# A selective scan on one NeuronCore: sums of y placed by a table, ScalarE's rows of B's diagonals in other steps, one GpSimd build a triple earlier

## The chip, the cores and the metric

The kernel runs on one core of one Trainium2 chip. The metric is the device time of one execution in microseconds (us). The kernel before took 1583.36 us, the median of three runs (1574.06 to 1601.38). The profiled execution, from which all rows below come, took 1595.89 us.

## The reference, cut to what matters

The model is one vision-Mamba block and one mixture-of-experts block on an input of 4 x 32 x 32 x 384. The change touches only the selective scan of the first block. With 192 channels, 16 states, 1024 positions and 4 directions, the reference computes for each image and direction

```python
def step(h, inp):
    u_t, d_t, B_t, C_t = inp
    dA = jnp.exp(d_t[..., None] * As)
    h = h * dA + (d_t * u_t)[..., None] * B_t[:, :, None, :]
    y = jnp.einsum('bkcn,bkn->bkc', h, C_t)
    return (h, y)
```

where d is softplus of a projection of the input (dt), u the convolved input, and B and C projections of it. Directions 2 and 3 run backwards, directions 1 and 3 over the transposed image. The outputs of the four directions are added into one y per image; then come a layer norm, a gate, a projection and the experts.

## The kernel before, in words

**Three stages.** A head (normalisation, projection, convolution; up to about 188 us of the span), the scan (`scan`, about 188 to 1315 us), and a tail (projection and experts). Only the scan is touched.

**Units and steps.** The scan works through 16 units, one for each image (4), orientation (2) and direction of flow (2); `unit_of` gives the three. A unit has 24 steps: 8 pairs of states, called triples here because each takes three steps (`CG = 3`), one for each group of 64 channels by 2 states by 1024 positions. So step i of a unit belongs to triple i // 3, part i % 3. "Step 3" in this text is step 3 of a unit, "unit 6" is the seventh. In one step:

- TensorE's `spread_b` (matmuls of line 1018) writes the term dt * u * B of the step into one of two PSUM buffers `s_pb`: 32 matmuls, 64 instructions, of the stationary dt * u with a diagonal matrix that holds B. It waits until the scan two steps back has ended (`h_ready`).
- ScalarE's `decay` (line 1109) writes exp(dt * A) into one of four buffers `s_a`, two steps ahead.
- VectorE's `step_h` (line 1183) does the scan itself, h = a * h + b along 1024 positions, into a ring of four triples of `s_h`.
- GpSimd's `times_c` (line 1219) multiplies h by C's row, two parts of a triple in one instruction and the third in another, in place.
- TensorE's `add_y` (line 1058) adds the products into y in PSUM (`s_py`, `s_py2`): the "sum" of the step. It waits for GpSimd (`hc_ready`) and for the sum before it. A slot of the ring is free for the scan when its sums are done (`y_added`).

**Order on each engine.** Each engine runs its instructions in program order, so the loops in the blocks of `scan` are the schedule: what waits holds all that stands behind it on the same engine. On TensorE, step i is: spread of step i, then the sums due by the function `summed`, then a carry if one is due, then the chunk of the next unit if one is due.

**Sums.** `summed(u, i)` says how many sums are done after step i of unit u: all up to seven steps back (`LAG = 7`). In even units after the first, `BEHIND` holds one or two more back in steps 7 to 12. This makes one sum a step, none in steps 7 and 8 of an even unit, two in steps 10 and 13 there.

**Carries.** At the middle of an image (after its first two units, one orientation), VectorE's `take_y` copies y out with the skip term (lines 1174 and 1175, after the scan of step 6), and TensorE adds it back transposed in six pieces, `carry` (lines 1028 and 1035), at the places of `CARRIES`: pairs of unit % 4 and step. At the end of an image ScalarE's `take_y` (line 1114 and the one after it, in step 6 of the next image's first unit) copies y out and SyncE's `store_y` stores it, in its queue behind the load of C's row for triple 3 and ahead of that for triple 4.

**Chunks.** During a unit, the inputs of the next are made: TensorE writes a chunk into the one bank `m_pm`, ScalarE takes it. Z chunks (dt before softplus, line 224) in steps 0 to 3, BT (line 228) in step 4, UT (u transposed, lines 237 and 239; only for even next units, so during odd ones) in steps 5, 7, 10 and 13, DUP (dt per channel group, line 245) in steps 16 to 19. The dt chunk of the prediction is the Z chunk. Softplus is done in three rounds from steps 7, 10 and 13 (`ROUND_AT`): ScalarE's logarithm (line 1095) into `m_pm`, then VectorE's two operations after the scan of the step (lines 1157 and 1160) and two after the next (1163 and 1166). After the scan of step 15 VectorE multiplies dt by u (`times_u`, line 308).

**Diagonals of B.** The 16 diagonal matrices of a unit stand in `k_area` in four quarters ("pieces"), which spreads read in steps 0 to 5, 6 to 11, 12 to 17 and 18 to 23. ScalarE builds pieces 0 and 2 a row at a time (`build_rows`, line 298; 32 rows of a piece): piece 0 of the next unit in steps 6 to 17, the first half of its piece 2 in steps 18 to 23, the second half in steps 0 to 5 of the unit itself, two or three rows a step. GpSimd builds pieces 1 and 3 in one instruction each (`build_d`, line 204): piece 3 of the unit behind triple 1, piece 1 of the next unit behind triple 4.

Of the kernel before, what the change touches and what calls it, by code (L numbers as in the profile page):

```python
# [40 lines left out]
BLK = 8  # L41
# [1 line left out]
CROWS = 3  # L43
TRIPLES = 4
LAG = 7
BEHIND = {LAG: 1, LAG + 1: 2, LAG + 2: 2, LAG + 3: 1, LAG + 4: 1, LAG + 5: 1}
CARRIES = {(2, 11): 0, (2, 12): 1, (2, 14): 2, (2, 15): 3, (3, 8): 4, (3, 11): 5}
ROUND_AT = (7, 10, 13)
ROUNDS = 3
AHEAD = 2  # L50
LN2 = 0.693147
LOG_MAX = 80.0
Y_STORED = 16 * 3
# [851 lines left out]
def scan(nc, d, keep, ys, m, norm, shared):  # L905

    with ExitStack() as ctx:
# [94 lines left out]
        @block.tensor  # L1002
        def _(pe):
            def spread_b(u, i):

                n, g = i // CG, i % CG
                step = u * STEPS + i
                if i == 0:
                    pe.wait_ge(dtu_ready, u + 1)
                if i % 6 == 0:  # L1010
                    piece = i // 6
                    pe.wait_ge(d_odd if piece % 2 else d_even, 2 * u + piece // 2 + 1)
                need(pe, h_ready, step - 1)
                for blk in range(BLK):
                    for r in range(2):
                        here = slice(r * HALF, (r + 1) * HALF)
                        for par in range(2):
                            mm = pe.matmul(pb[par * HALF:(par + 1) * HALF, step % 2, r * BANK + blk:(r + 1) * BANK:BLK],  # L1018
                                           dtut[here, u % 2, blk, g * HALF:(g + 1) * HALF], dd[here, 2 * n + par, blk],
                                           start=True, stop=True)  # L1020
                mm.then_inc(b_row, 1)

            def carry(b, piece, made):

                pe.wait_ge(y_added, made)
                if piece < 4:
                    q, w = halves()[piece // 2], piece % 2
                    mm = pe.matmul(py[:, q].rearrange("p (w h) -> p w h", h=HW)[:, w * HW // 4:(w + 1) * HW // 4], eye[:],
                                   y01[:].rearrange("p (h w) -> p w h", w=HW)[:, piece * HW // 4:(piece + 1) * HW // 4],
                                   start=False, stop=False)  # L1030
                else:
                    for x in range(2):
                        lh = x ^ (piece - 4)
                        here, cols = slice(lh * HALF, (lh + 1) * HALF), slice(x * HW // 2, (x + 1) * HW // 2)
                        mm = pe.matmul(py2[x * HALF:(x + 1) * HALF].rearrange("p (w h) -> p w h", h=HW)[:, :, lh * HW // 2:(lh + 1) * HW // 2],
                                       eye[here, here], y2[here].rearrange("p (h w) -> p w h", w=HW)[:, cols], start=False, stop=False)
                mm.then_inc(y_carried, 1)
                pe.wait_ge(y_carried, len(CARRIES) * b + piece + 1)

            def add_y(n, part):  # L1040

                b, o, s = unit_of(n // NP)
                first, last = n % (2 * NP) == 0, n % (2 * NP) == 2 * NP - 1
                if first and part == 0:
                    need(pe, y_taken, 2 * taken(b, o))
                at = n % TRIPLES * CG
                pe.wait_ge(hc_ready, 2 * n + (1 if part == 0 else 2))
                need(pe, y_added, CG * n + part)
                for r in range(2):
                    here = slice(r * HALF, (r + 1) * HALF)  # L1050
                    into = (part + r) % CG
                    opens, closes = first and part == (0, 0, 1)[into], last and part == (2, 1, 2)[into]
                    for x in range(2):
                        if into < 2:
                            dst, src = py[x * HALF:(x + 1) * HALF, halves()[into]], h[here, at + x, halves()[into]]
                        else:
                            dst, src = py2[x * HALF:(x + 1) * HALF], h[here, at + 2, halves()[x]]
                        mm = pe.matmul(dst, eye[here, here], src, start=opens, stop=closes)  # L1058
                mm.then_inc(y_added, 1)

            def summed(u, i):

                held = u > 0 and u % 2 == 0
                return max(0, u * STEPS + i + 1 - LAG - (BEHIND.get(i, 0) if held else 0))

            for u in range(UNITS):
                for i in range(STEPS):
                    step = u * STEPS + i
                    spread_b(u, i)
                    made = summed(u, i)  # L1070
                    for at in range(summed(u, i - 1), made):
                        add_y(at // CG, at % CG)
                    if (u % 4, i) in CARRIES:
                        carry(u // 4, CARRIES[u % 4, i], made)
                    if u + 1 < UNITS:
                        for what in chunks_of(u + 1):
                            if chunk_slot(*what) == i:
                                m.chunk(pe, u + 1, *what)
                    elif 6 <= i < 6 + TT:
                        t = i - 6  # L1080
                        if t == 0:
                            pe.wait_ge(norm.y_in, 16)
                            pe.wait_ge(chunk_taken, len(CHUNK))
                        need(pe, norm.yt_taken, t)
                        norm.turn(pe, pm, t)
            for step in range(LAST - LAG, LAST):
                add_y(step // CG, step % CG)

        @block.scalar
        def _(act):  # L1090
            def logarithm(u, r):
# [1 line left out]
                act.wait_ge(chunk_taken, CHUNK[u, "BT", 0] + 1 + (r + 2 if u % 2 == 0 else 0))  # L1093
                need(act, dt_ready, ROUNDS * u + r)
                nc.scalar.activation(pm[:], ez[:, round_cols(r)], ACT.Ln, bias=1.0).then_inc(ln_ready, 1)

            def share(k):

                return 4 * BLK * k // 12

            def decay(step):
                u, i = step // STEPS, step % STEPS
# [17 lines left out]
            for u in range(UNITS):  # L1120
                b, o, s = unit_of(u)
                for i in range(STEPS):
                    step = u * STEPS + i
                    if step + AHEAD < LAST:
                        decay(step + AHEAD)
                    if i == 6 and s == 0 and o == 0 and u:
                        take_y(b - 1)
                    if u + 1 < UNITS:
                        for what in chunks_of(u + 1):
                            if chunk_slot(*what) == i:  # L1130
                                m.take_chunk(act, u + 1, *what)
                        if 4 <= i < 6:
                            m.exponent(act, u + 1, i - 3)
                        if i in ROUND_AT:
                            logarithm(u + 1, ROUND_AT.index(i))
                        if 6 <= i < 18:
                            m.build_rows(act, u + 1, 0, share(i - 6), share(i - 5))
                        if i >= 18:
                            m.build_rows(act, u + 1, 2, share(i - 18), share(i - 17))
                    if i < 6:  # L1140
                        m.build_rows(act, u, 2, share(i + 6), share(i + 7))
                    if u == LAST_U and 6 <= i < 6 + TT:
                        norm.take(act, pm, 0, i - 6).then_inc(norm.yt_taken, 1)
            norm.root(act, 0)
# [4 lines left out]
        def _(dve):  # L1149
# [36 lines left out]
            for u in range(UNITS):  # L1186
                b, o, s = unit_of(u)
                for i in range(STEPS):
                    step_h(u * STEPS + i)
                    if i == 6 and s == 0 and o == 1:  # L1190
                        take_y(b)
                    if u + 1 < UNITS:
                        for r, at in enumerate(ROUND_AT):
                            if at <= i < at + 2:
                                softplus(u + 1, r, 2 * (i - at))
                                softplus(u + 1, r, 2 * (i - at) + 1)
                        if i == 15:
                            m.times_u(dve, u + 1)
                    if u == LAST_U and i == 0:
                        nc.vector.memset(norm.eps[:], 1e-5).then_inc(norm.eps_ready, 1)  # L1200
                    if u == LAST_U and 8 <= i < 8 + TT:
# [11 lines left out]
        def _(pool):  # L1213
# [8 lines left out]
            for u in range(UNITS):  # L1222
                for n in range(NP):
                    times_c(u * NP + n, range(0, 2))
                    times_c(u * NP + n, range(2, CG))
                    if n == 1:
                        m.build_d(pool, nc.gpsimd.tensor_tensor, u, 3)
                    if n == 4 and u + 1 < UNITS:
                        m.build_d(pool, nc.gpsimd.tensor_tensor, u + 1, 1)


# [661 lines left out]
```

## Time and profile before

| | busy us | share of the span |
|---|---|---|
| span of the profiled execution | 1594.1 | (execution: 1595.89) |
| PE, TensorE matmul | 1351.7 | 85% |
| DVE, VectorE | 1229.5 | 77% |
| POOL, GpSimd | 1025.6 | 64% |
| ACT, ScalarE | 1018.5 | 64% |
| line 1183, the 384 scans | 862.4 | 2275 ns each |
| line 1219, the products with C | 880.1 | 3468 ns each |
| line 1018, spreads | 479.2 | 226 ns a matmul instruction |
| line 1058, sums | 431.7 | 614 ns a matmul instruction |

How to read it: shares are over the whole span, of which the scan is some 1120 us. A busy time of matmuls that follow each other without a gap overlaps, because each instruction's time holds its fill and drain; for TensorE the distance from one start to the next says more than the durations. The rows of a timeline merge equal instructions that follow each other; the brackets tell how long the engine was idle before them and which engine's work ended that; "issue" stands where no releaser is seen. The granted clock of TensorE is given as a share: 1.00 is 2.4 GHz, 0.50 is 1.2 GHz. Units 1 to 14 are the stretch from 263.61 to 1244.45 us.

### The profile page before, as it was taken

The numbers are of one execution on the slowest core, as the hardware profiler recorded it, in microseconds if no ns is written. First come the engines' busy times: TensorE is split into PE (matmuls) and PEld (weight loads), VectorE is DVE, ScalarE is ACT, GpSimd is POOL, SyncE is SP. The second block draws the span as 40 slices with busy tenths as digits, with TensorE's granted clock in tenths as the row PEclk, the third lists the DMA queues.
The fourth block names the chain that finished last, engine by engine and source line by source line (L and its number), as shares of the span: only waits on it lengthen the run. The fifth ranks groups of instructions, "written<-read, shape, count | busy, mean of one in ns | idle before, by whom it ended". The sixth has DMA issues, their size and how long they took to land. (4 is left out here: it accounts for less than half of the span.)

```text
span 1594.1 us, 66411 instructions
## 1 busy us (share of the span) xinstructions
PE 1351.7 (85%) x30388; PEld 830.5 (52%) x30388; DVE 1229.5 (77%) x1029; ACT 1018.5 (64%) x1957; POOL 1025.6 (64%) x294
## 2 busy tenths in 40 slices
PE   6997688888987888998788899878889886969998
PEld 5734455554554555555555555545555543535554
DVE  4876198989899898989989997997989884644220
ACT  3448677777778778787877877776787551311222
POOL 0002089989899998999899998988899980000000
PEclk8998879999999999999999999998999997789999
DMA  9243524233333423333342332334243326100111
GB/s 324 97 156 145 170 56 112 76 93 82 81 87 89 109 79 93 79 90 81 89 113 78 91 99 70 85 85 109 66 101 80 97 82 221 67 0 35 40 40 45
DMA packets 73479, 151.13 MB, mean 95 GB/s; under 512 B 33238, under 2 KB 41942, under 8 KB 72816
## 3 DMA queue, kind: packets, MB, share of 16 engines
q1 hardware_dynamic: 73200, 146.88, 32.1%
q8 instruction: 240, 3.93, 1.1%
q14 instruction: 39, 0.32, 0.1%
HBM read 101.76 MB, written 32.51 MB: 84 GB/s over the span
## 5 line engine op out<-in xcount | busy, mean ns | idle before, releaser
L1219 POOL TENSOR_TENSOR s_h<-s_h,s_crow 128x2048 f32<-128x2048 f32 (+1 forms) x256 | 880.1, 3468 | 159.3 <-DVE s_h L1183 159.3
L1183 DVE TENSOR_TENSOR_SCAN s_h<-s_a,s_pb 128x1024 f32<-128x1024 f32 x384 | 862.4, 2275 | 131.7 <-PE s_pb L1018 96.3
L1018 PE MATMUL s_pb<-k_area,m_dtut 64*64 64x64 f32 x24576 | 479.2, 226 | 149.6 <-DVE s_h L1183 98.7
L1018 PEld LDWEIGHTS s_pb<-k_area,m_dtut 64*64 64x64 f32 x24576 | 435.4, 139 | 325.1 <-DVE s_h L1183 161.9
L1058 PE MATMUL s_py<-s_h,k_eye 64*64 64x512 f32 x3072 | 431.7, 614 | 14.6 <-issue 8.3
L298 ACT ACTIVATE k_area<-k_mask,m_bt 128x64 f32<-128x64 f32 x992 | 273.3, 337 | 0.0
L1109 ACT ACTIVATE s_a<-y_y,m_aneg 128x1024 f32<-128x1024 f32 x192 | 219.0, 1142 | 54.1 <-DVE s_h L1183 53.9
L1109 ACT ACTIVATE s_a<-m_dup,m_aneg 128x1024 f32<-128x1024 f32 x192 | 219.3, 1143 | 32.5 <-DVE s_h L1183 32.5
L204 POOL TENSOR_TENSOR k_area<-m_bt,k_mask 128x2048 f32<-128x2048 f32 x33 | 145.0, 4396 | 128.9 <-ACT m_bt L273 128.9
L1058 PEld LDWEIGHTS s_py<-s_h,k_eye 64*64 64x64 f32 x3072 | 93.2, 138 | 41.4 <-issue 35.6
L270 ACT COPY y_y<-m_pm 128x384 f32<-128x384 f32 x60 | 28.8, 479 | 79.0 <-PE m_pm L224 79.0
L224 PEld LDWEIGHTS m_pm<-k_wdt,k_rows 25*128 25x128 f32 x256 | 43.2, 199 | 59.7 <-issue 59.3
L224 PE MATMUL m_pm<-k_wdt,k_rows 25*128 25x192 f32 x256 | 63.7, 372 | 7.2 <-DMA k_rows<-scratch_xd 7.2
L1504 PE MATMUL t_small<-t_w,k_area 128*128 128x384 f32 x192 | 69.1, 497 | 0.0
L1478 PE MATMUL t_big<-t_xn,t_w 128*128 128x512 f32 x144 | 68.2, 625 | 0.0
L1568 ACT COPY t_out<-t_small 128x384 f32<-128x384 f32 x32 | 15.3, 479 | 82.4 <-PE t_small L1507 82.4
L819 DVE SCALAR_TENSOR_TENSOR h_acc<-h_xpad,h_conv_p,h_acc 128x1024 f32<-128x1024 f32 x48 | 61.7, 1285 | 1.6
L245 PEld LDWEIGHTS m_pm<-k_eye,y_y 64*64 64x64 f32 (+1 forms) x512 | 33.5, 123 | 52.7 <-issue 47.2
L1692 DVE TENSOR_TENSOR k_area<-k_area,t_big 128x1024 f32<-128x1024 f32 x12 | 14.3, 1220 | 47.9 <-PE t_big L1492 47.7
L1504 PEld LDWEIGHTS t_small<-t_w,k_area 128*128 128x128 f32 x192 | 36.5, 194 | 18.2 <-issue 1.2
L245 PE MATMUL m_pm<-k_eye,y_y 64*64 64x64 f32 (+1 forms) x512 | 43.0, 224 | 2.9 <-ACT y_y L273 2.7
L1478 PEld LDWEIGHTS t_big<-t_xn,t_w 128*128 128x128 f32 x144 | 27.8, 200 | 32.4 <-issue 31.9
(190 smaller groups left out, 1234.3 us busy)
## 6 DMA issues: line engine op xcount, KB each, us to landing
s_crow<-scratch_xd SPq DMA_DIRECT2D x256, 256.0 KB, 4.1
k_area<-in_x_dram SPq DMA_DIRECT2D x4, 1536.0 KB, 7.9
scratch_xt<-y_y SPq DMA_DIRECT2D x4, 1536.0 KB, 8.6
y_y<-y_y SPq DMA_DIRECT2D x24, 256.0 KB, 4.3
m_dup<-m_dup SPq DMA_DIRECT2D x24, 256.0 KB, 4.2
out_dram<-t_out SPq DMA_DIRECT2D x32, 192.0 KB, 1.9
k_area<-scratch_xt SPq DMA_DIRECT2D x3, 1536.0 KB, 6.8
scratch_xd<-h_dbl SPq DMA_DIRECT2D x8, 512.0 KB, 2.6
```

What stands on the lines that cost most here:

```text
L204: tt(self.dd[:, rows_n].rearrange("p n k j -> p (n k) j"), self.bt[:, u % 2, rows_n].rearrange("p n k -> p (n k)").unsqueeze(2).broadcast_ ...
L224: mm = pe.matmul(pm[:, x * DI:(x + 1) * DI], tokens(rows[0:R + 1], 2 * i + x), self.keep["wdt"][:, o + 2 * s], start=True, stop=True)
L245: mm = pe.transpose(pm[0:chans.stop - chans.start, blk::BLK], self.dt_of[here, blk, chans], eye[here, here])
L298: row = self.nc.scalar.activation(self.dd[:, n, blk], self.keep["mask"][:], ACT.Identity, scale=self.bt[:, u % 2, n, blk:blk + 1])
L819: eng.scalar_tensor_tensor(out, view, w, out, ALU.mult, ALU.add).then_inc(convolved[kind], 1)
L1018: mm = pe.matmul(pb[par * HALF:(par + 1) * HALF, step % 2, r * BANK + blk:(r + 1) * BANK:BLK], dtut[here, u % 2, blk, g * HALF:(g + 1) * H ...
L1058: mm = pe.matmul(dst, eye[here, here], src, start=opens, stop=closes)
L1109: nc.scalar.activation(a[:, step % RING], dup[u % 2][:, g], ACT.Exp, scale=aneg[:, col:col + 1]).then_inc(a_ready, 1)
L1183: nc.vector.tensor_tensor_scan(h[:, step % (TRIPLES * CG), f], a[:, step % RING, f], pb[:, step % 2, f], 0.0, ALU.mult, ALU.add).then_inc( ...
L1219: nc.gpsimd.tensor_tensor(here, here, c.unsqueeze(1).broadcast_to([P, groups.stop - groups.start, L]), ALU.mult).then_inc(hc_ready, 1)
L1478: mm = pe.matmul(big_of("F1", b, j)[:, q], w1[:, c, j * P:(j + 1) * P], xn[:, b % 2, c, q], start=(c == 0), stop=(c == NC - 1))
L1504: pe.matmul(ps, hid[:, j, tok], w2[:, j], start=False, stop=False, skip_group_check=True)
```

## The change

Three tables replace `LAG` and `BEHIND`: how many sums follow the spread of each step, in the first unit (`SUMS_FIRST`), in odd units (`SUMS_ON`) and in the other even ones (`SUMS_NEW`). Steps 0 to 3 have none; at the end of a unit five sums are owed instead of seven. The carries move to steps 13 and 14 of the third unit of an image and 9, 11, 14 and 15 of its fourth. In steps 7, 10 and 13 the chunk stands ahead of the sums on TensorE. VectorE's `take_y` moves from behind the scan of step 6 to behind the softplus of step 7, ScalarE's from step 6 to step 8, behind the logarithm of step 7. ScalarE's rows stand in other steps. GpSimd's piece 1 of the next unit comes behind triple 3 instead of 4.

```diff
-BEHIND = {LAG: 1, LAG + 1: 2, LAG + 2: 2, LAG + 3: 1, LAG + 4: 1, LAG + 5: 1}
-CARRIES = {(2, 11): 0, (2, 12): 1, (2, 14): 2, (2, 15): 3, (3, 8): 4, (3, 11): 5}
+OWED = 5
+SUMS_NEW = {4: 1, 5: 1, 6: 2, 7: 1, 10: 1, 11: 2, 12: 1, 13: 2, 14: 2, 15: 2, 16: 1, 17: 1, 18: 1, 19: 1, 20: 1, 21: 1, 22: 2, 23: 1}
+SUMS_ON = {4: 1, 5: 1, 6: 1, 7: 1, 8: 2, 9: 1, 10: 1, 11: 2, 12: 1, 13: 1, 14: 2, 15: 2, 16: 1, 17: 1, 18: 1, 19: 1, 20: 1, 21: 1, 22: 1, 23: 1}
+SUMS_FIRST = {i: 1 for i in range(LAG - 1, STEPS)} | {15: 2}
+CARRIES = {(2, 13): 0, (2, 14): 1, (3, 9): 2, (3, 11): 3, (3, 14): 4, (3, 15): 5}
+TAKE_Y = 7
+ROWS_NEXT = {11: (0, 6), 12: (6, 9), 13: (9, 13), 14: (13, 20), 15: (20, 27), 16: (27, 30), 17: (30, 32)}
+ROWS_SOON = {20: (0, 4), 21: (4, 8), 22: (8, 12), 23: (12, 16)}
+ROWS_LATE = {6: (16, 18), 7: (18, 21), 8: (21, 27), 9: (27, 29), 10: (29, 32)}
...
-                held = u > 0 and u % 2 == 0
-                return max(0, u * STEPS + i + 1 - LAG - (BEHIND.get(i, 0) if held else 0))
+                plan = SUMS_FIRST if u == 0 else SUMS_ON if u % 2 else SUMS_NEW
+                return max(0, u * STEPS - OWED) + sum(count for at, count in plan.items() if at <= i)
+            def chunks_at(u, i):
+                for what in chunks_of(u + 1):
+                    if chunk_slot(*what) == i:
+                        m.chunk(pe, u + 1, *what)
...
                     spread_b(u, i)
+                    if u + 1 < UNITS and i in ROUND_AT:
+                        chunks_at(u, i)
                     made = summed(u, i)
...
-                    if u + 1 < UNITS:
-                        for what in chunks_of(u + 1):
-                            if chunk_slot(*what) == i:
-                                m.chunk(pe, u + 1, *what)
-                    elif 6 <= i < 6 + TT:
+                    if u + 1 < UNITS and i not in ROUND_AT:
+                        chunks_at(u, i)
+                    elif u == LAST_U and 6 <= i < 6 + TT:
...
-            for step in range(LAST - LAG, LAST):
+            for step in range(summed(LAST_U, STEPS - 1), LAST):
...
-                    if i == 6 and s == 0 and o == 0 and u:
+                    if i == TAKE_Y + 1 and s == 0 and o == 0 and u:
                         take_y(b - 1)
...
-                        if 6 <= i < 18:
-                            m.build_rows(act, u + 1, 0, share(i - 6), share(i - 5))
-                        if i >= 18:
-                            m.build_rows(act, u + 1, 2, share(i - 18), share(i - 17))
-                    if i < 6:
-                        m.build_rows(act, u, 2, share(i + 6), share(i + 7))
+                        if i in ROWS_NEXT:
+                            m.build_rows(act, u + 1, 0, *ROWS_NEXT[i])
+                        if i in ROWS_SOON:
+                            m.build_rows(act, u + 1, 2, *ROWS_SOON[i])
+                    if i in ROWS_LATE:
+                        m.build_rows(act, u, 2, *ROWS_LATE[i])
...
-                    if i == 6 and s == 0 and o == 1:
-                        take_y(b)
...
+                    if i == TAKE_Y and s == 0 and o == 1:
+                        take_y(b)
...
-                    if n == 4 and u + 1 < UNITS:
+                    if n == 3 and u + 1 < UNITS:
                         m.build_d(pool, nc.gpsimd.tensor_tensor, u + 1, 1)
```

## Rows read from the trace of the kernel before

**Rows 1.** Busy time of each engine in units 1 to 14 (instructions), granted clock, DMA

```profile
263.61:1244.45 980.84, 840.33 (x25316) 522.95 (x25312) 885.16 (x526) 756.00 (x1552) 891.83 (x254) 0.97 0.35 89
```

**Rows 2.** Who waited for whom in units 1 to 14: us in total, times, longest

```profile
DVE s_h L1183 <- PE s_pb L1018: 75.7, 108, 4.2
DVE m_pm L1157 <- ACT m_pm L1095: 12.6, 10, 2.3
...
POOL s_h L1219 <- DVE s_h L1183: 88.9, 55, 4.1
...
PE s_pb L1018 <- issue: 36.9, 41, 2.4
```

**Rows 3.** VectorE in time, unit 6: start us, duration us, line, operation, idle before

```profile
619.29 2.29 DVE L1183 TENSOR_TENSOR_SCAN s_h<-s_a,s_pb 128x1024 f32<-128x1024 f32 x1 [0.51 <-PE s_pb L1018]
...
639.35 0.67 DVE L1163 SCALAR_TENSOR_TENSOR m_pm<-y_y,m_pm 128x512 f32<-128x512 f32 x1
...
640.66 4.46 DVE L1183 TENSOR_TENSOR_SCAN s_h<-s_a,s_pb 128x1024 f32<-128x1024 f32 x2
...
662.90 8.81 DVE L1183 TENSOR_TENSOR_SCAN s_h<-s_a,s_pb 128x1024 f32<-128x1024 f32 x4
```

**Rows 4.** TensorE in time, unit 6, steps 1 and 4: start us, duration us

```profile
615.27 1.16 PE L1018 MATMUL s_pb<-k_area,m_dtut 64*64 64x64 f32 x64
616.25 1.04 PE L1058 MATMUL s_py<-s_h,k_eye 64*64 64x512 f32 x8
617.22 0.91 PE L224 MATMUL m_pm<-k_wdt,k_rows 25*128 25x192 f32 x4
618.07 1.16 PE L1018 MATMUL s_pb<-k_area,m_dtut 64*64 64x64 f32 x64
...
625.61 0.67 PE L228 MATMUL m_pm<-k_eye,k_rows 16*128 16x16 f32 x8
626.20 1.16 PE L1018 MATMUL s_pb<-k_area,m_dtut 64*64 64x64 f32 x64
```

**Rows 5.** TensorE in time, units 6 and 7: carry, second sum, DUP and UT chunks

```profile
645.11 1.11 PE L1028 MATMUL s_py<-y_y,k_eye 128*128 128x256 f32 x2
646.27 1.16 PE L1018 MATMUL s_pb<-k_area,m_dtut 64*64 64x64 f32 x64
...
650.53 1.04 PE L1058 MATMUL s_py<-s_h,k_eye 64*64 64x512 f32 x8
651.75 1.09 PE L1058 MATMUL s_py<-s_h,k_eye 64*64 64x512 f32 x8 [0.18 <-PE s_py L1058]
...
661.11 0.71 PE L245 MATMUL m_pm<-k_eye,y_y 64*128 64x64 f32 x8
661.75 1.16 PE L1018 MATMUL s_pb<-k_area,m_dtut 64*64 64x64 f32 x64
...
697.07 0.39 PE L237 MATMUL m_pm<-k_eye,k_u 64*64 64x64 f32 x4
...
698.28 1.16 PE L1018 MATMUL s_pb<-k_area,m_dtut 64*64 64x64 f32 x64
```

**Rows 6.** TensorE in time: stops in steps 0 to 2, units 2 and 13

```profile
332.88 0.34 PE L1018 MATMUL s_pb<-k_area,m_dtut 64*64 64x64 f32 x5 [1.14 <-issue]
...
1098.50 1.08 PE L1058 MATMUL s_py<-s_h,k_eye 64*64 64x512 f32 x4 [1.94 <-issue]
```

**Rows 7.** Engines and clock in stretches of units 0, 2, 13; VectorE in units 0, 13

```profile
193.85:211.57 17.72, 17.02 (x405) 15.01 (x404) 11.49 (x6) 14.27 (x29) 9.61 (x3) 0.50 0.20 51
...
352.00:355.40 3.40, 1.84 (x91) 1.56 (x91) 3.40 (x4) 3.40 (x8) 3.40 (x3) 1.00 0.02 5
...
1099.70:1109.80 10.10, 10.10 (x153) 6.00 (x152) 3.90 (x2) 4.99 (x11) 6.92 (x3) 0.50 0.23 56
...
202.87 2.29 DVE L1183 TENSOR_TENSOR_SCAN s_h<-s_a,s_pb 128x1024 f32<-128x1024 f32 x1 [1.20 <-PE s_pb L1018]
...
1108.19 2.29 DVE L1183 TENSOR_TENSOR_SCAN s_h<-s_a,s_pb 128x1024 f32<-128x1024 f32 x1 [2.91 <-PE s_pb L1018]
```

**Rows 8.** GpSimd in time, unit 6, triple 4: start us, duration us, idle before

```profile
654.46 6.87 POOL L1219 TENSOR_TENSOR s_h<-s_h,s_crow 128x2048 f32<-128x2048 f32 x2 [2.32 <-DVE s_h L1183]
```

More of the change, by code:

```diff
@@ L1095, in logarithm @@
                 nc.scalar.activation(pm[:], ez[:, round_cols(r)], ACT.Ln, bias=1.0).then_inc(ln_ready, 1)
-            def share(k):
-                return 4 * BLK * k // 12
             def decay(step):
```

## The prediction, made before the result was known

> **What bounds the kernel now.** I read the busy time of the engines over units 1 to 14 first, then who waited for whom there, then the instructions of VectorE and TensorE in time, then TensorE's granted clock. In these 980.84 us VectorE is busy 885.16 and GpSimd 891.83 [rows 1]: 63.2 and 63.7 us of the 70.06 that a unit takes. VectorE lacks 95.7 us; 75.7 of them end with TensorE's spread of B, 12.6 with ScalarE's logarithm [rows 2]. So VectorE sets the pace, TensorE delays it, and GpSimd lies one short step below: GpSimd's own 88.9 of waits are all for scans [rows 2]; if all waits of VectorE went, its 891.8 would be the floor, 89 us less.
>
> Where the waits lie is seen in time. Four scans without a gap take 8.81 us, 2.20 each; in the first steps of a unit each scan has 0.51 of idle time before it [rows 3]. TensorE there takes 2.80 a step: spread 0.98, sum 0.97, dt chunk 0.85 [rows 4]. In the later steps spread and sum fit. In steps 7, 8, 10, 11, 13 and 14 two softplus operations lengthen VectorE's step by 1.31 [rows 3], to 3.5; there TensorE has room. A spread needs 1.16 and may start when the scan two steps back has ended, so 0.85 of lateness (2.20 less 1.16 and some 0.2 for signals, an estimate) is hidden, and 1.3 more for each softplus pair on either side.
>
> **Sums by a table.** The number is unchanged, 24 a unit; they move. Steps 0 to 3 fall from 2.80 to 1.83 us of TensorE, below 2.20: the 0.51 goes, four times a unit, and most of the 0.26 behind the BT chunk (0.59 [rows 4]): 2.3 x 14 = 32. In odd units the UT chunk of step 5 adds 1.21 [rows 5]; that step is 0.98 + 0.97 + 1.21, some 0.85 above a scan's, all of it idle time now; with 0.85 hidden, the 0.35 that step 4 leaves over is what will be idle: 3 less for seven units. Together **-35**.
>
> What is late next: a second sum in a step costs 1.22, a carry 1.16 and a later start of 0.15 to 0.25 for the operation before it [rows 5]. Step 14 of units 3, 7 and 11 has spread, two sums and a carry: 0.98 + 1.22 + 0.97 + 1.4 = 4.5 against a scan step of 2.2, step 15 the same against 3.5, and steps 16 to 19 have a DUP chunk of 0.64 each [rows 5] on top of 1.9, against 2.2 once the softplus is over. The lateness reaches about 4.5 and is hidden up to 3.9: summed step by step some 2.5 of idle a unit. Units 2, 6, 10 and 14 (carries in 13 and 14) 0.6. Together **+10**; bounds 3 (every signal as short as the shortest) and 15.
>
> Each sum now runs up to two steps later or earlier against GpSimd. At step 23 the sum of triple 6, part 0, is wanted as its product ends; in odd units the same holds at 17 and 20. A late product holds the spread behind it on TensorE's queue, then VectorE. Steps 0 to 3 give back 0.4 each: **+2**, bounds 0 and 14 (1 us in each unit).
>
> **The clock.** TensorE stops inside spreads for 36.9 us, 41 times, with no engine as releaser [rows 2]. The code has no wait there. The same instructions run beside the same transfers after the change, so I keep the stops. In four of the 14 units (2, 7, 11 and 13) one lies in steps 0 to 2, of which the first and the last stand in [rows 6]. After three of them the clock falls to 1.2 GHz, in unit 13 for 10.1 us [rows 7]. Now sums stand in those steps, and the clock came back behind sums. In unit 0 TensorE does spreads and dt chunks without sums, the very mix of the new steps 0 to 3: it was busy 17.02 of 17.72 us and stayed at 0.50 throughout; each scan waited 1.20 [rows 7]. So a clock that falls in steps 0 to 3 will stay down until the sums of step 4. Price of such a unit: three steps x 1.20, then step 4 at the low clock, between 1.20 and the 2.91 that a slow step with a sum costs [rows 7], taken as 2.3, and a part of step 5, 0.8: 6.7 (bounds 3.6 and 9.4). Four units: 27. They pay today: about four slow steps, each 2.91 - 0.51 = 2.4 above the regular wait: 10. Net **+17**; with no fall -10, with every unit +84.
> In even units steps 8 and 9 have no sum either. Softplus covers them, but a fallen clock reaches the double sums of 11 and 13: **+4** (bounds 0 and 12).
>
> **The edits beside it.** Chunks ahead of sums in steps 7, 10 and 13 give ScalarE the UT chunk 0.97 sooner, against ten waits for the logarithm of 1.26 on average [rows 2]; the other cause in some units, ScalarE's copy of y ahead of the logarithm of step 7, moves to step 8. Of 12.6, **-11** (bounds 0 and -12.6). Its own new wait is for the last sum, now at step 7; behind it stand only decays two steps ahead, and behind SyncE's store of y, which waits for it, the load of C's rows for triple 4, needed some 20 us later: 0.
> VectorE's copy of y moves behind the softplus of step 7: the same work, 0. ScalarE's rows out of steps 0 to 5: no scan waits for a decay in these units [rows 2], 0 either way; 3 to 7 rows fall on long steps. GpSimd's quarter, now behind triple 3, fills the 2.32 for which it waits before triple 4 [rows 8]; what it needs, spread 11, is long done. 0; without this cover triple 4 is some 3 us late, which is the case of late products below.
> Unit 0 (one sum earlier), unit 15 and five instead of seven sums left at the end: **-2**, bounds 0 and -5.
>
> Sum: -35 + 10 + 2 + 17 + 4 - 11 - 2 = **-15**. The profiled execution took 1595.89 (span 1594.1 and 1.8 around it), so 1581 by it. It lies 12.5 above the median of the three runs, 1583.36; on that median I forecast **1568**.
>
> **Rivals.** (a) The clock holds through steps 0 to 3. For it: TensorE stays busy 1.83 of 2.2 us there, and unit 2's stretch of spreads alone kept 1.00 with TensorE busy for 1.84 of 3.40 [rows 7]; stops might fall in other steps. Against: [rows 6]. Then -35 + 7 - 10 + 1 - 11 - 2 = -50: 1533; with two falling units 1546.
> (b) Slower: short idle times in each of steps 0 to 3 let the clock fall in nearly every unit, and nothing raises it until step 4. The chain: 14 x 6.7 - 10 = +84 in place of +17, and 4 becomes 8: +56, 1639; each falling unit costs 6.7, so it decides from 12 falling units on (1621). For it: unit 0. Against: unit 0 began at the low clock and never fell from the high one. The Trainium skill, TensorE: Matmul & The Clock Gate, section "A second HAM failure mode: psum-queue depth-cycling", tells of a kernel whose small idle times between groups of matmuls made the clock swing; by that rule the time is (b)'s, and the 1.00 of unit 2's spreads [rows 7] does not agree.
> (c) GpSimd becomes the bound: its 63.7 a unit is only 0.5 over VectorE's floor; if the sums at 17, 20 and 23 wait for late products in every unit, +30 instead of +2: 1596.
> (d) The second and third edit move nothing that anyone waits for: that is in the sum, except the -11 for the logarithm; without it 1579.
>
> **Numbers.** This measurement tells about 2% (32 us) from no change. Chances: the forecast with three to eight falling units, (d) included, 0.47, 1553 to 1600; (a) 0.33, 1526 to 1551; (c) 0.09; (b) 0.11. Faster by over 2% is (a) with a little of the forecast's lower end, less (a)'s upper end: 0.33; slower is (b): 0.11; the rest 0.56. The range leaves out the lower end of (a) (no fall and carries at their lower bound) and (b): 1533 to 1604.
>
> **What will show it.** Right: 0.51 gone from steps 1 to 4 in most units; VectorE's wait for the logarithm below 3 us; in a few units a clock of 0.50 from a stop in steps 0 to 2 until step 5 with waits of 1.20 a scan; waits of some 2.5 in steps 14 to 20 of units 3, 7 and 11. Wrong: no clock under 1.00 in steps 0 to 3 (then (a)), 0.50 there in every unit (then (b)), or sums that wait for GpSimd for more than 1 us a unit (then (c)).

## The result: slower by 2.4%

The kernel after takes 1626.12 us (median; 1610.66 to 1628.72), the kernel before beside it 1586.62: a ratio of 1.0238, interval 1.0191 to 1.0285. The forecast was 1568, range 1533 to 1604. A ratio in this text compares only those executions of a kernel that lie within 1.5% of its quickest, so it can differ from the ratio of the medians. The profiled execution took 1625.52 us (span 1623.7) against 1595.89.

The busy times of units 1 to 14, now 263.34 to 1272.95, answer to [rows 1]; columns: length; PE, PEld, DVE, ACT, POOL busy (instructions); granted clock; DMA share; GB/s.

```profile
263.34:1272.95 1009.61, 892.26 (x25307) 571.46 (x25305) 901.09 (x527) 752.04 (x1546) 870.95 (x253) 0.92 0.34 87
```

These units are 28.8 us longer than before, nearly all of the 29.6 by which the span grew. The same work keeps VectorE busy 15.9 us longer and GpSimd 20.9 us shorter, and the clock is 0.92 instead of 0.97. Who waited for whom there (us in total, times, longest) answers to [rows 2]:

```profile
POOL s_h L1227 <- DVE s_h L1191: 137.1, 66, 4.2
DVE s_h L1191 <- PE s_pb L1025: 105.3, 115, 3.9
...
PE s_pb L1025 <- issue: 37.4, 34, 2.9
...
PEld s_py L1065 <- POOL s_h L1227: 11.3, 11, 1.0
```

VectorE's wait for the logarithm (12.6 before) has no row any more. Its wait for spreads has grown from 75.7 to 105.3. TensorE's stops are unchanged in sum. GpSimd waits more, so it is not the bound. Where VectorE's busy time went is in the groups of instructions by line, of the same stretches (busy us, mean ns of one | idle before). Before, VectorE's and GpSimd's:

```profile
L308 DVE TENSOR_TENSOR m_dtut<-y_y,m_ut 128x1536 f32<-128x1536 f32 x14 | 24.2, 1732 | 0.0
...
L204 POOL TENSOR_TENSOR k_area<-m_bt,k_mask 128x2048 f32<-128x2048 f32 x28 | 123.3, 4403 | 0.0
```

After:

```profile
L315 DVE TENSOR_TENSOR m_dtut<-y_y,m_ut 128x1536 f32<-128x1536 f32 x14 | 39.7, 2837 | 0.0
...
L211 POOL TENSOR_TENSOR k_area<-m_bt,k_mask 128x2048 f32<-128x2048 f32 x28 | 101.7, 3633 | 0.0
```

The product dt * u (`times_u`, line 308 before, 315 after) takes 1.1 us longer, once a unit: 15.5 us. GpSimd's builds take 0.77 less, 21.6 in all. Neither instruction was changed; only the build's place was. The two engines in time show why; VectorE and GpSimd before, unit 6:

```profile
661.25 1.73 DVE L308 TENSOR_TENSOR m_dtut<-y_y,m_ut 128x1536 f32<-128x1536 f32 x1
...
661.28 5.18 POOL L204 TENSOR_TENSOR k_area<-m_bt,k_mask 128x2048 f32<-128x2048 f32 x1
```

and GpSimd, VectorE and TensorE after, unit 13 from the end of triple 3 to step 19:

```profile
1162.47 3.64 POOL L211 TENSOR_TENSOR k_area<-m_bt,k_mask 128x2048 f32<-128x2048 f32 x1
1166.05 6.90 POOL L1227 TENSOR_TENSOR s_h<-s_h,s_crow 128x2048 f32<-128x2048 f32 x2
...
1171.63 2.93 DVE L315 TENSOR_TENSOR m_dtut<-y_y,m_ut 128x1536 f32<-128x1536 f32 x1
1174.49 6.63 DVE L1191 TENSOR_TENSOR_SCAN s_h<-s_a,s_pb 128x1024 f32<-128x1024 f32 x3
1182.23 2.29 DVE L1191 TENSOR_TENSOR_SCAN s_h<-s_a,s_pb 128x1024 f32<-128x1024 f32 x1 [1.12 <-PE s_pb L1025]
...
1176.91 1.81 PE L1025 MATMUL s_pb<-k_area,m_dtut 64*64 64x64 f32 x64 [2.47 <-DVE s_h L1191]
1178.43 2.00 PE L1065 MATMUL s_py<-s_h,k_eye 64*64 64x512 f32 x8
```

Before, dt * u began 0.03 us ahead of the quarter's build and ran its 1.73; the build, alone 3.63, took 5.18: longer by about one dt * u. After, the build is done early, GpSimd's products run until 1172.95, and dt * u, issued at 1171.63, ends 1.6 us behind that. Whichever starts first runs, the other waits, and the wait shows as a longer instruction, not as idle time. The build, GpSimd's products and dt * u all read two operands from SBUF. The scans and softplus operations beside GpSimd keep their 2.28 and 0.67 to 0.70; they take one operand from PSUM. The Trainium skill, SBUF — State Buffer, section "SBUF: two separate sides", has this as a rule: VectorE and GpSimd share a port pair that is "an exclusive lock, not a bandwidth split", VectorE needs it when it reads two SBUF inputs, and the first to start keeps it for the whole instruction. The rows agree.

The scan behind dt * u is late in turn, TensorE idles 2.47 us for it, and its clock falls behind that; the engines' busy times and clock:

```profile
1177.20:1180.60 3.40, 3.40 (x71) 1.79 (x63) 3.40 (x2) 0.75 (x1) 3.40 (x1) 0.50 0.95 231
```

The next spread takes 1.81 instead of 1.16 and the sum 2.00 instead of 1.04, and the scan of step 19 waits 1.12. In seven of units 1 to 14 the clock falls between steps 17 and 19. The waits at step 19 grew from 1.2 to 11.0 us over these units.

The rest is at the start of the units. Unit 2, no fall: VectorE has nearly no gap.

```profile
335.13 8.96 DVE L1191 TENSOR_TENSOR_SCAN s_h<-s_a,s_pb 128x1024 f32<-128x1024 f32 x4 [0.19 <-PE s_pb L1025]
```

Unit 4, after a stop of TensorE in step 1, in VectorE's and TensorE's instructions, and the engines' busy times and clock of the stretch:

```profile
484.05 2.29 DVE L1191 TENSOR_TENSOR_SCAN s_h<-s_a,s_pb 128x1024 f32<-128x1024 f32 x1 [1.20 <-PE s_pb L1025]
487.54 2.29 DVE L1191 TENSOR_TENSOR_SCAN s_h<-s_a,s_pb 128x1024 f32<-128x1024 f32 x1 [1.20 <-PE s_pb L1025]
492.13 2.29 DVE L1191 TENSOR_TENSOR_SCAN s_h<-s_a,s_pb 128x1024 f32<-128x1024 f32 x1 [2.30 <-PE s_pb L1025]
...
476.33 0.91 PE L1025 MATMUL s_pb<-k_area,m_dtut 64*64 64x64 f32 x43 [1.19 <-issue]
```

```profile
477.00:494.50 17.50, 17.50 (x343) 13.03 (x335) 11.43 (x5) 10.04 (x14) 12.57 (x4) 0.51 0.24 63
```

These rows answer to [rows 6] and [rows 7]. The stretch is at 1.2 GHz to its end, TensorE is busy all of it, and scans wait 1.20 each, 2.30 when the sums come back. Seven units look so (3, 4, 7, 9, 11, 12, 14).

Summed over units 1 to 14 from the brackets of VectorE's timeline, its waits for spreads are, before and after: steps 0 to 7, 55.8 and 68.3; steps 12 to 18, 0 and 3.3; step 19, 1.2 and 11.0; steps 20 to 23, 18.7 and 22.7. That is +29.6. With +15.5 for dt * u and -12.6 for the logarithm, -5.0 for VectorE's idle time ahead of the first scan of unit 15, which only the stretch of before holds, and +1.3 of small items, it makes the 28.8. VectorE and TensorE before, then both after:

```profile
1244.45 2.29 DVE L1183 TENSOR_TENSOR_SCAN s_h<-s_a,s_pb 128x1024 f32<-128x1024 f32 x1 [5.05 <-PE s_pb L1018]
...
1240.75 1.11 PE L1058 MATMUL s_py<-s_h,k_eye 64*64 64x512 f32 x1 [3.24 <-issue]
...
1270.75 2.29 DVE L1191 TENSOR_TENSOR_SCAN s_h<-s_a,s_pb 128x1024 f32<-128x1024 f32 x1 [3.89 <-PE s_pb L1025]
...
1270.34 0.34 PE L1025 MATMUL s_pb<-k_area,m_dtut 64*64 64x64 f32 x8 [2.90 <-issue]
```

Both follow a stop of TensorE at the end of unit 14. After the change it falls one step earlier, and its 3.9 us are the whole growth of steps 20 to 23.

### The profile page after: what moved, and what is told of

Read it like the earlier page. It is cut to its first block and busy times, and to the rows that moved or that the text cites. A ratio compares the mean times of both kernels' runs of the same rounds, so it can differ in the third digit from the quotient of the medians.

```text
span 1623.7 us, 66415 instructions
## 1 busy us (share of the span) xinstructions
PE 1401.2 (86%) x30388; PEld 875.4 (54%) x30388; DVE 1246.6 (77%) x1029; ACT 1016.6 (63%) x1957; POOL 1003.3 (62%) x294
## 5 line engine op out<-in xcount | busy, mean ns | idle before, releaser
L1025 PEld LDWEIGHTS s_pb<-k_area,m_dtut 64*64 64x64 f32 x24576 | 462.0, 146 | 293.0 <-issue 157.1
L1025 PE MATMUL s_pb<-k_area,m_dtut 64*64 64x64 f32 x24576 | 500.2, 232 | 118.6 <-DVE s_h L1191 71.3
L1065 PE MATMUL s_py<-s_h,k_eye 64*64 64x512 f32 x3072 | 442.6, 634 | 20.6 <-PE s_py L1065 12.3
L305 ACT ACTIVATE k_area<-k_mask,m_bt 128x64 f32<-128x64 f32 x992 | 261.1, 336 | 0.0
L211 POOL TENSOR_TENSOR k_area<-m_bt,k_mask 128x2048 f32<-128x2048 f32 x33 | 122.0, 3698 | 128.3 <-ACT m_bt L280 128.3
L231 PE MATMUL m_pm<-k_wdt,k_rows 25*128 25x192 f32 x256 | 74.9, 423 | 10.4 <-DMA k_rows<-scratch_xd 7.8
L277 ACT COPY y_y<-m_pm 128x384 f32<-128x384 f32 x60 | 28.8, 479 | 81.4 <-PE m_pm L231 81.0
L231 PEld LDWEIGHTS m_pm<-k_wdt,k_rows 25*128 25x128 f32 x256 | 51.3, 231 | 19.2 <-issue 13.7
L315 DVE TENSOR_TENSOR m_dtut<-y_y,m_ut 128x1536 f32<-128x1536 f32 x16 | 45.2, 2824 | 8.2 <-ACT m_ut L280 8.2
```

The source lines that it names most:

```text
L211: tt(self.dd[:, rows_n].rearrange("p n k j -> p (n k) j"), self.bt[:, u % 2, rows_n].rearrange("p n k -> p (n k)").unsqueeze(2).broadcast_ ...
L231: mm = pe.matmul(pm[:, x * DI:(x + 1) * DI], tokens(rows[0:R + 1], 2 * i + x), self.keep["wdt"][:, o + 2 * s], start=True, stop=True)
L305: row = self.nc.scalar.activation(self.dd[:, n, blk], self.keep["mask"][:], ACT.Identity, scale=self.bt[:, u % 2, n, blk:blk + 1])
```

## The experiments

**Which part costs: the quarter or the sums?** The theory: GpSimd's instructions against dt * u; the rival: the clock in steps 0 to 3. Three kernels beside the same runs of before (1587.91). First the kernel after with the quarter back:

```diff
-                    if n == 3 and u + 1 < UNITS:
+                    if n == 4 and u + 1 < UNITS:
```

> The changed kernel with GpSimd's quarter behind triple 4 again. Theory A: behind triple 3 the quarter makes GpSimd's products run when VectorE comes to its product dt * u (1.73 us each before, 2.84 after), which costs 14 x 1.1 = 15.5 us, and the clock that falls in TensorE's idle time meanwhile costs another 9.8 at step 19 (the profile of after). Then dt * u takes 1.73 again, no scan waits at step 19, and the time is 1.003 to 1.010 of the kernel before. Rival B: the sums, their doubles and the carries cost it all and the quarter nothing: 1.02 or more, dt * u still near 2.8.

1.014 (1.0070 to 1.0209), 1617.3 us, more than the expected 1.003 to 1.010. This did not isolate the collision: dt * u took 1.73 in nine units, but 4.60 to 5.15 in the other five. Here is one, VectorE and GpSimd:

```profile
449.79 5.13 DVE L315 TENSOR_TENSOR m_dtut<-y_y,m_ut 128x1536 f32<-128x1536 f32 x1
...
449.70 3.61 POOL L211 TENSOR_TENSOR k_area<-m_bt,k_mask 128x2048 f32<-128x2048 f32 x1
```

The build began 0.09 us ahead, and VectorE waited for its end. Before, dt * u led by 0.03; the new sums had shifted the two by a tenth of a microsecond. Next the kernel before with nothing but the quarter moved:

```diff
-                    if n == 4 and u + 1 < UNITS:
+                    if n == 3 and u + 1 < UNITS:
```

> The kernel before with only GpSimd's quarter moved behind triple 3. Theory A: dt * u meets the second product of triple 4 and takes 2.7 to 3.2 us; with the fallen clock behind it 15 to 25 us more: 1.009 to 1.016 of before. Rival B: the quarter fills idle time of GpSimd and nothing changes: 0.998 to 1.002, dt * u 1.73.

1.0154 (1.0110 to 1.0197), 1613.25 us: two thirds of the loss from the edit that was costed at nothing. VectorE, GpSimd and TensorE, unit 6:

```profile
670.20 2.90 DVE L308 TENSOR_TENSOR m_dtut<-y_y,m_ut 128x1536 f32<-128x1536 f32 x1
680.77 2.29 DVE L1183 TENSOR_TENSOR_SCAN s_h<-s_a,s_pb 128x1024 f32<-128x1024 f32 x1 [1.13 <-PE s_pb L1018]
...
664.62 6.86 POOL L1219 TENSOR_TENSOR s_h<-s_h,s_crow 128x2048 f32<-128x2048 f32 x2
...
675.44 1.74 PE L1018 MATMUL s_pb<-k_area,m_dtut 64*64 64x64 f32 x64 [2.08 <-DVE s_h L1183]
```

The same picture in all 14 units, 2.87 to 2.93 each: 16.4 us longer, and 14.4 us of waits at step 19 (before 1.2). Third, the order of chunks, the copies of y and ScalarE's rows alone, with the sums, the carries and the quarter of before:

```diff
-                plan = SUMS_FIRST if u == 0 else SUMS_ON if u % 2 else SUMS_NEW
-                return max(0, u * STEPS - OWED) + sum(count for at, count in plan.items() if at <= i)
+                held = u > 0 and u % 2 == 0
+                return max(0, u * STEPS + i + 1 - LAG - (BEHIND.get(i, 0) if held else 0))
...
-                    if n == 3 and u + 1 < UNITS:
+                    if n == 4 and u + 1 < UNITS:
```

> The changed kernel with the sums, carries and GpSimd's quarter of before: what is left is the chunk ahead of the sum in steps 7, 10 and 13, both copies of y behind the softplus or logarithm of step 7, and ScalarE's rows in other steps. Theory: the 12.6 us for which VectorE waited for the logarithm go and nothing comes in their place: 0.990 to 0.994 of before. Rival: what is won there comes back as a wait of the sums for the copied y at step 9 or as a wait of TensorE for the softplus at steps 10 and 13: 0.998 to 1.003.

0.9946 (0.9918 to 0.9973), 8.6 us by the ratio. The wait for the logarithm is gone, as in the kernel after.

**Do sums hold the clock up?** The kernel with the quarter back, and two sums moved into steps 1 and 3:

```diff
-SUMS_NEW = {4: 1, 5: 1, 6: 2, 7: 1, 10: 1, ...}
-SUMS_ON = {4: 1, 5: 1, 6: 1, 7: 1, 8: 2, 9: 1, ...}
+SUMS_NEW = {1: 1, 3: 1, 5: 1, 6: 1, 7: 1, 10: 1, ...}
+SUMS_ON = {1: 1, 3: 1, 6: 1, 7: 1, 8: 2, 9: 1, ...}
```

> The first kernel of this set (quarter back) with one sum in steps 1 and 3 of each unit, taken from steps 4 and 6 or 4 and 5. Theory C: once the clock has fallen in steps 0 to 2, only sums bring it back; with sums at 1 and 3 a low stretch at a unit's start lasts 3 to 7 us instead of 9 to 14, and waits of 1.20 a scan last one or two steps; 15 to 25 us less than the first kernel of this set. Rival D: the stops themselves cost the time and the clock only comes with them: equal to the first kernel within 5 us, or slower by some 5 for the fuller steps 1 and 3.

0.9996 (0.9958 to 1.0033) against 1.014. Idle time in steps 0 to 7 fell from 59.9 to 40.8 us, and no stretch at 1.2 GHz there exceeds 10.2 us (17.5 after). Here sums in the early steps shorten the low stretches, and the time falls with them. But dt * u collided in three units instead of five, some 6 us of the gain, so the size is not clean.

**dt * u out of GpSimd's way.** The kernel after, with the product one scan later:

```diff
-                        if i == 15:
+                        if i == 16:
                             m.times_u(...)
```

> The changed kernel as it is, GpSimd's quarter behind triple 3, with VectorE's product dt * u behind the scan of step 16 instead of 15. Theory A: dt * u takes 1.73 when it starts ahead of a GpSimd instruction and otherwise waits for that instruction's end and then takes 1.65. Behind scan 16 GpSimd has ended triple 4 and waits for this very scan, so VectorE is first: 14 x 1.1 = 15.5 us and most of the 9.8 at step 19 go; 1.008 to 1.013 of the kernel before. Rival B: the sums cost it all and dt * u is long for another reason: 1.020 or more, dt * u above 2.5.

1.0020 (0.9985 to 1.0055): 2.2 points of the 2.4 are gone, more than expected. dt * u takes 1.73 in all but one unit, where it took 6.53. Waits at step 19 are 0; new are 9.4 us at step 16, 2.2 each in units 3, 7 and 11, where the carries lost the cover of dt * u, and 0.7 each in units 2, 6, 10 and 14. By the two traces units 1 to 14 are 28.9 us shorter. The collision is 21.7 of that: 10.7 in dt * u and 11.0 at step 19. Steps 0 to 7 idle 48.9 instead of 68.3 too, which the place of dt * u does not explain, and steps 16 and 20 to 23 give most of that back.

The same with the sums in steps 1 and 3, by the tables of the experiment before:

```diff
-                        if i == 15:
+                        if i == 16:
                             m.times_u(...)
...
+SUMS_NEW = {1: 1, 3: 1, 5: 1, 6: 1, 7: 1, 10: 1, ...}
+SUMS_ON = {1: 1, 3: 1, 6: 1, 7: 1, 8: 2, 9: 1, ...}
```

> The kernel above (dt * u behind scan 16) with one sum in steps 1 and 3. No product of GpSimd meets dt * u in either, so the pair differs in the sums alone. Theory C (without sums a fallen clock stays down): 15 to 25 us less than the kernel above, 0.992 to 0.999 of before, and no low stretch over 7 us in steps 0 to 5. Rival D (the stops cost the time, the clock only comes with them): within 5 us of the kernel above.

1.0056 (1.0025 to 1.0088). The expected 15 to 25 us did not come: in five units dt * u came to lie behind the last product of triple 4 and the first of triple 5 and took 6.7 to 6.8 there, some 25 us against 4.8 in the kernel above. Steps 0 to 7 idle 38.8 instead of 48.9. The collision hides what the clock gave: inconclusive.

The kernel before, with the quarter moved and dt * u behind scan 16:

```diff
-                        if i == 15:
+                        if i == 16:
                             m.times_u(...)
...
-                    if n == 4 and u + 1 < UNITS:
+                    if n == 3 and u + 1 < UNITS:
```

> The kernel before with GpSimd's quarter behind triple 3 and dt * u behind scan 16: neither the sums nor ScalarE's rows are changed. Theory A: the quarter's move costs nothing once dt * u is out of its way: 0.998 to 1.002 of before, against 1.015 with the quarter alone; dt * u 1.73. Rival: the move costs 1.5% by itself, as the quarter makes triple 4 late: 1.010 or more.

0.9955 (0.9932 to 0.9979) where the quarter alone cost 1.0154. So the quarter's move costs nothing if dt * u is not in its way. The two moves together even gain; no run moves dt * u alone in the kernel before, so which of them gains is not shown. VectorE and GpSimd, unit 6:

```profile
663.22 1.73 DVE L308 TENSOR_TENSOR m_dtut<-y_y,m_ut 128x1536 f32<-128x1536 f32 x1
664.87 6.63 DVE L1183 TENSOR_TENSOR_SCAN s_h<-s_a,s_pb 128x1024 f32<-128x1024 f32 x3
...
651.87 3.62 POOL L204 TENSOR_TENSOR k_area<-m_bt,k_mask 128x2048 f32<-128x2048 f32 x1
...
663.44 12.76 POOL L1219 TENSOR_TENSOR s_h<-s_h,s_crow 128x2048 f32<-128x2048 f32 x3 [1.13 <-DVE s_h L1183]
```

dt * u leads by 0.22 us, and now GpSimd's products pay: three take 12.76, where they take 11.4 undisturbed. GpSimd has the room: the time did not grow.

Last in this group, the kernel after with dt * u behind scan 16 and sums in steps 0, 2 and 3:

```diff
-SUMS_NEW = {4: 1, 5: 1, 6: 2, 7: 1, 10: 1, ...}
-SUMS_ON = {4: 1, 5: 1, 6: 1, 7: 1, 8: 2, 9: 1, ...}
+SUMS_NEW = {0: 1, 2: 1, 3: 1, 6: 1, 7: 1, 10: 1, ...}
+SUMS_ON = {0: 1, 2: 1, 3: 1, 6: 1, 7: 1, 8: 1, 9: 1, ...}
```

> As the second kernel of this set, with sums in steps 0, 2 and 3 and none in 1, 4 and 5, where BT and UT chunks stand: a search for a version that beats both kernels. Theory C: clock as with sums in 1 and 3, steps 4 and 5 fit: 0.988 to 0.996 of before. Rival: the full steps 2 and 3 give back the 0.5 of idle a scan, and it is equal to the second kernel or slower by up to 8 us.

1.0031 (0.9977 to 1.0085), and 1.3% slower by the medians (1608.41 and 1587.24); 0.988 to 0.996 was expected. In its trace no stretch at 1.2 GHz at a unit's start exceeds 6.8 us and steps 0 to 7 idle 39.9 us, the lowest but one of all. Yet the time is no better than with sums from step 4 on. So of the three kernels with sums in the early steps only the first is quicker than its partner, and what the clock is worth in time stays open. That trace is the quickest of its executions (1580.52, median 1608.41), so it does not show where the rest of the time goes.

**The table of sums by itself.** Two kernels that differ by the sums and the carries alone: all other edits and dt * u behind scan 16, with the sums of before, and with those of after (the second is the version above, run again).

```diff
-                plan = SUMS_FIRST if u == 0 else SUMS_ON if u % 2 else SUMS_NEW
-                return max(0, u * STEPS - OWED) + sum(count for at, count in plan.items() if at <= i)
+                held = u > 0 and u % 2 == 0
+                return max(0, u * STEPS + i + 1 - LAG - (BEHIND.get(i, 0) if held else 0))
```

> The kernel after with dt*u behind scan 16, but with the sums and carries of before. If the two small gains add up (sum order, copies and rows alone 0.9946; the quarter with dt*u moved 0.9955), 0.990 of the kernel before, 1571 us for 1587; it would be the first version that beats both. Rival: both gains take away the same wait of VectorE (in steps 7 to 16), then 0.995. dt*u 1.73 us in 13 or more of 14 units, the wait for the logarithm 0 to 2 us over units 1 to 14, idle before scans in steps 0 to 7 some 50 to 58 us.

> The kernel after with dt*u behind scan 16, again, beside the run with the sums of before: the two differ by the table of sums and the carries alone. If the table costs by itself, 1.002 of the kernel before and 1.008 to 1.013 of the other run, with stretches at 1.2 GHz of over 10 us at the start of 4 to 7 units. Rival: the table costs nothing once dt*u is out of GpSimd's way, and the earlier 1.002 against 0.9955 was that run's chance: then within 0.004 of the other run.

With the sums of before 0.9904 (0.9870 to 0.9937), 1573.52 us: the two small gains add up, and this version beats both kernels. With those of after 1.0015 (0.9965 to 1.0066), 1598.03 us. So the table costs 1.1% by the two ratios (1.0015 / 0.9904), and 1.6% by the medians. The trace of the second has one collision left, in unit 12: 4.9 us, or 0.3%, which leaves a cost. The rival, that the table costs nothing without the collision, falls. The waits of units 1 to 14 tell where; with the sums of before:

```profile
DVE s_h L1188 <- PE s_pb L1022: 73.6, 101, 2.9
PEld s_py L1062 <- POOL s_h L1224: 5.1, 5, 1.0
```

with those of after:

```profile
DVE s_h L1191 <- PE s_pb L1025: 85.9, 83, 4.2
PEld s_py L1065 <- POOL s_h L1227: 19.7, 19, 1.2
```

By steps: 57.2 becomes 46.1 in steps 0 to 7, but 0.5 becomes 9.5 at step 16, and 15.5 becomes 27.6 in steps 20 to 23, where sums that stand five instead of seven steps behind the scan wait for GpSimd's products and an even unit has a double sum. Of the 27.6, 4.2 are the stop at the end of unit 14, which in the first of the two falls outside the stretch; so these steps grew by about 8. Step 16 of unit 3, VectorE and TensorE:

```profile
450.91 2.29 DVE L1191 TENSOR_TENSOR_SCAN s_h<-s_a,s_pb 128x1024 f32<-128x1024 f32 x1 [2.21 <-PE s_pb L1025]
453.12 1.73 DVE L315 TENSOR_TENSOR m_dtut<-y_y,m_ut 128x1536 f32<-128x1536 f32 x1
...
447.39 1.09 PE L1065 MATMUL s_py<-s_h,k_eye 64*64 64x512 f32 x8 [0.18 <-POOL s_h L1227]
448.56 1.06 PE L1042 MATMUL s_py<-y_y,k_eye 64*64 64x256 f32 x4
449.68 1.16 PE L1025 MATMUL s_pb<-k_area,m_dtut 64*64 64x64 f32 x64
```

As [rows 5] has them singly, a sum, a second sum and a carry stand ahead of the spread, and nothing on VectorE covers them. Where dt * u stood behind scan 15, it did.

## Why the prediction was wrong, by its own steps

**GpSimd's quarter, costed at 0: the step that failed.** The prediction named what the build needs and the idle time it fills, and looked for late products. It did not ask what the build had kept away. Before, in each of these units dt * u won by hundredths of a microsecond over a build; with the build gone it met a product that was already running. The collision stood in the trace of before: one build of a unit took 5.18 us, and the mean of 4.40 puts the other at 3.6. The idle time of [rows 8] that the build was to fill was there, and did not matter. Measured: +15.5 in dt * u and some +10 at step 19, and, when dt * u moves away, 2.2 points of time with the sums (1.0238 to 1.0020) and 2.0 without (1.0154 to 0.9955).

**The clock, +17: the price was right, the count was not.** Falls come behind stops, they last until the sums of steps 4 and 5, and scans wait 1.20, all as written. But seven units fell for long, not four. They idle 7.6 us each in steps 0 to 7, of which some 0.9 is there without a stop (see the table of sums below): 6.7, as forecast. Rival (b) needed twelve units. It gives 1621 to 1639, and the measured 1626 lies there, but by luck: seven units fell, and much of the time came from dt * u.

The prediction kept the stops in their steps. Their sum stayed, but their places follow the order of TensorE's instructions. Counted along its instructions in the trace (matmuls, weight loads and semaphore instructions), the stops of over 0.7 us in units 1 to 14, 23 before and 25 after, all lie a whole multiple of 256 instructions apart, to within one. These units hold 200 such places, and some 40 of them show a stop; a new order puts other steps there. Why one place stops and another does not stays open, and with it why seven units fell; the same table showed five such units with dt * u moved, in one trace.

**Sums by a table, -35: too large.** Without a stop, steps 0 to 7 idled 1.8 us in an even unit before (unit 4: three waits of 0.51, not four, and one of 0.26) and 3.1 in an odd one (unit 3). After, they idle 1.0 (unit 10) and 0.8 (unit 1). That is 0.8 and 2.3 less, 1.5 on average; the forecast was 2.5. The 0.51 of [rows 3] went, but the double sum of step 6 in even units, never priced, leaves 0.4 to 0.9 at step 7, and 0.8 stayed at step 6 of odd units, where the forecast left 0.35 (its step 5 is 0.96 above a scan's, not 0.85). An estimate from these four units: in steps 0 to 7 the table gave -22 instead of -35, and stops with the clock +34 instead of +17. That is the difference between -18 forecast for these steps and +12.5.

**Carries, +10, and late products, +2.** In the kernel after the carries cost 3.3 in steps 12 to 18, since dt * u stood there as cover, and late products next to nothing: the 4.0 more in steps 20 to 23 are the stop at the end of unit 14. With dt * u moved, 9.0 and about 8: near the forecast, and within its bounds of 0 and 14.

**The logarithm, -11:** -12.6, and by itself 0.9946. Right, so (d) fell. **(a)** fell with the clock, and **(c)** since GpSimd waits 137.1 us.

## What to carry to other kernels

Before an instruction of GpSimd is moved, list VectorE's instructions with two SBUF inputs, and see which of the two engines starts first now and which will then; an instruction whose duration differs between two places of one program is the sign. A short operation on the critical engine belongs where the other engine is idle or has just finished, with more than a few hundredths of a microsecond of margin. A cost that is hidden is hidden by something in particular, and each table of the order has to be priced at every step that it makes longer, not only at those that it makes shorter.

## What was not expected of the hardware

The side that waits is not always served between two instructions of the other. In the last kernel dt * u took 6.65 us in unit 12, VectorE and GpSimd:

```profile
1078.94 6.65 DVE L315 TENSOR_TENSOR m_dtut<-y_y,m_ut 128x1536 f32<-128x1536 f32 x1
...
1072.60 11.37 POOL L1227 TENSOR_TENSOR s_h<-s_h,s_crow 128x2048 f32<-128x2048 f32 x3
```

The three products ran without a gap (4.55, 2.37 and 4.55 undisturbed), so dt * u was issued in the second, waited for the third as well, and ended at 1085.6, 1.6 us behind it. In unit 4 of the same trace it was issued in the same product, which ended at 519.67, and was served next:

```profile
519.30 1.98 DVE L315 TENSOR_TENSOR m_dtut<-y_y,m_ut 128x1536 f32<-128x1536 f32 x1
...
519.61 6.07 POOL L1227 TENSOR_TENSOR s_h<-s_h,s_crow 128x2048 f32<-128x2048 f32 x1
```

Here the product behind it took 6.07 instead of 4.55. The four kernels with the new sums and dt * u behind scan 16 show 15 such meetings in units 1 to 14: in eight dt * u waited for the second product too (6.5 to 6.8 us), in seven it came between (2.0 to 2.3). What decides is not shown.
